# Values two to a step in odd pairs, a copied-out reciprocal, and the sums of a cross-attention folded on GpSimd

## The reference

```
x: (4, 256, 256)   context: (4, 4096, 256)   8 heads of 64
q  = ln(x) @ Wq1;  k, v = [ln(x) @ Wk1, context @ Wk2], [ln(x) @ Wv1, context @ Wv2]
attn = softmax(q k^T / 8 over 256 + 4096 keys);  out = (attn @ v) @ Wo + bo
```

## Time and profile before

| | |
|---|---|
| median of three runs | 1646.91 us (1642.55, 1646.91, 1647.23) |
| the profiled execution | 1643.33 us, its span 1641.8 us |
| mean granted TensorE clock | 0.962 of full speed |
| busy share of the span | TensorE 88%, VectorE 68%, GpSimd 64%, ScalarE 44% |
| units 1 to 14 of the cross-attention | from 131 to 1094 us of the span |
| the last unit | from 1094.4 to 1147.2 us |

### The profile page before, as it was taken

One profiled execution on the slowest core, in us unless ns is written; L12 is line 12 of the kernel. 1 busy time (PEld: TensorE's weight loads), 2 busy tenths in 40 slices (PEclk: granted clock), 3 DMA queues, 4 the chain that ended last, 5 costly groups with the idle time before them and its releaser, 6 DMA issues. The chain is left out here.

```text
span 1641.8 us, 27858 instructions
## 1 busy us (share of the span) xinstructions
PE 1449.9 (88%) x10964; PEld 1068.2 (65%) x10964; DVE 1124.3 (68%) x1299; ACT 728.3 (44%) x971; POOL 1049.4 (64%) x541
## 2 busy tenths in 40 slices
PE   4999999999999999999999999996597777827995
PEld 4767766776776776677677667664354444517995
DVE  2797578658658756855875785684776999644663
ACT  3454445534444544443554344342345333224773
POOL 3385469838547864754885665477134999443885
PEclk8999999999999999999999999998798999958998
DMA  5000021000003000001200000000304800092333
GB/s 176 14 11 11 1 87 49 1 14 21 2 27 88 24 2 14 21 1 39 88 11 14 10 11 1 1 2 1 85 19 190 214 0 1 1 368 62 63 60 59
DMA packets 62382, 76.39 MB, mean 47 GB/s; under 512 B 6384, under 2 KB 47984, under 8 KB 61856
## 3 DMA queue, kind: packets, MB, share of 16 engines
q1 hardware_dynamic: 57168, 68.51, 13.7%
q0 software_dynamic: 5088, 6.11, 2.5%
HBM read 58.39 MB, written 17.25 MB: 46 GB/s over the span
## 5 line engine op out<-in xcount | busy, mean ns | idle before, releaser
L393 POOL TENSOR_TENSOR xa_prob_sum<-xa_prob_sum,xa_probs 128x1024 f32<-128x1024 f32 x240 | 573.5, 2389 | 177.9 <-ACT xa_probs L481 158.7
L552 DVE TENSOR_REDUCE xa_maxes<-psum 128x2 f32<-128x1024 f32 (+1 forms) x288 | 334.2, 1162 | 240.1 <-PE psum L753 238.3
L481 ACT ACTIVATE xa_probs<-xa_probs 128x1024 f32<-128x1024 f32 x272 | 288.6, 1061 | 429.1 <-DVE xa_probs L574 428.8
L574 DVE TENSOR_TENSOR xa_probs<-psum,xa_max_rows 128x1024 f32<-128x1024 f32 x272 | 330.3, 1216 | 14.8 <-PE psum L784 8.5
L796 PE MATMUL psum<-xa_probs,xa_vals 128*64 128x256 f32 x2176 | 280.9, 389 | 4.0 <-ACT xa_probs L481 2.8
L796 PEld LDWEIGHTS psum<-xa_probs,xa_vals 128*64 128x64 f32 x2176 | 137.8, 136 | 106.4 <-issue 42.9
L780 PE MATMUL psum<-xa_q_hi,xa_k_hi 64*128 64x256 f32 x1088 | 158.8, 285 | 0.8 <-DVE xa_probs L574 0.8
L678 PE MATMUL psum<-xa_wv_hi,xa_ctx_hi 128*128 128x256 f32 x512 | 150.9, 295 | 7.8 <-DVE xa_maxes L552 7.8
L784 PE MATMUL psum<-xa_q_hi,xa_k_lo 64*128 64x256 f32 x1088 | 155.3, 279 | 0.0
L782 PE MATMUL psum<-xa_q_lo,xa_k_hi 64*128 64x256 f32 x1088 | 155.2, 279 | 0.0
L753 PE MATMUL psum<-xa_k_hi,xa_q_hi 64*128 64x512 f32 (+1 forms) x604 | 136.0, 452 | 21.4 <-DVE xa_maxes L552 9.3
(11 more groups left out here) (329 smaller groups left out, 2887.0 us busy)
## 6 DMA issues: line engine op xcount, KB each, us to landing
xa_ctx_in<-in_ctxT_dram SPq DMA_DIRECT2D x32, 512.0 KB, 4.6
ex_slots<-mx_blank_tile SPq DMA_DIRECT2D x2, 4372.5 KB, 38.4
xa_stage<-in_L_xattn_Wk_dram SPq DMA_DIRECT2D x32, 128.0 KB, 2.4
xa_stage<-in_L_xattn_Wv_dram SPq DMA_DIRECT2D x16, 256.0 KB, 3.0
ex_raw<-in_L_ffn_w_gate_dram SPq DMA_DIRECT2D x8, 512.0 KB
ex_raw<-in_L_ffn_w_up_dram SPq DMA_DIRECT2D x8, 512.0 KB
ex_raw<-in_L_ffn_w_down_dram SPq DMA_DIRECT2D x8, 512.0 KB
ex_xt<-ex_slots SPq DMA_DIRECT2D x15, 265.0 KB, 3.1
```

What stands on the lines that cost most here:

```text
L393: pool.tensor_tensor(prob_sum[:, :], prob_sum[:, :], probs[:, n % RING, :], ALU.add).then_inc(summed, 1)
L481: nc.scalar.activation(probs[:, n % RING, :], probs[:, n % RING, :], ACT.Exp, scale=HD ** -0.5).then_inc(exp_done, 1)
L552: dve.tensor_reduce(maxes[:, qt, :, g:g + 1], max_banks(v, g, qt)[:, :, 0:group_keys(g)[1]], AX_X, ALU.max).then_inc(max_reduced, 1)
L574: dve.tensor_tensor(probs[:, n % RING, :].rearrange("p (h t q) -> p h t q", h=2, t=2), S[:, 2 * (n % 2):2 * (n % 2) + 2, :].rearrange("p h ...
```

## The change

- `v_due`: an odd unit now makes 16 values in the steps 1 to 8, the even unit after it only the last one, in step 0.
- TensorE: in odd units `project_keys(v, d+1)` goes behind the values, to the end of the step, and both `weigh` stand ahead of the values. In step 8 the values stand ahead of `weigh(u, 16)`. In step 0 `sum_probs(u-1)` stands ahead of the value and of `project_keys(v, 1)`.
- VectorE: in odd units `split_keys(v, d)` stands behind the first `reduce_max` of the step, ahead of `shift(u, 2d)`. The reciprocal and `normalize` are taken in step 0 of even units, and in the steps 1 and 2 of odd ones. `split_q` stands ahead of `store_max`.
- The reciprocal comes from SBUF: ScalarE copies the bank O as a whole to `raw` (`store_outputs`, in step 0 between the two exponentials); `weigh(u, 0)` waits for this copy alone. `normalize` then has both its inputs in SBUF.
- GpSimd folds `prob_sum` in half once per unit (`fold_sums`, behind the last `add_probs`), so that `sum_probs` has two matmuls in place of four.
- In the last unit VectorE adds up every third tile (1, 4, 7, 10, 13, 16) by itself in `late_sum`; GpSimd adds the other eleven, unfolded, and `sum_probs` sums both.

```diff
+def late(j):
+    return j % 3 == 1
 def sums_done(n):
...
-    return n // HG * (HG - 1) + max(1, n % HG)
+    u, j = n // HG, n % HG
+    if u == U - 1:
+        return u * (HG - 1) + max(1, sum(not late(i) for i in range(j + 1)) - 1)
+    return u * (HG - 1) + max(1, j)
+def late_done(j):
+    return sum(late(i) for i in range(j + 1))
...
         prob_sum = sb("xa_prob_sum", [P, 2 * 2 * N1])
-        inv_sum = sb("xa_inv_sum", [P, N1])
+        raw = sb("xa_raw", [P, 2, N1])
         heads_T = sb("xa_heads_T", [P, IC, N1])
...
         bo_sb = heads_T[:, 0, :]
+        late_sum = xl_next[:, 0:4, :].rearrange("p t d -> p (t d)")
...
             if u % 2 == 1 and u + 1 < U:
-                return [((u + 1) // 2, j) for j in (2 * d - 4, 2 * d - 3) if 0 <= j]
+                return [((u + 1) // 2, j) for j in (2 * d - 2, 2 * d - 1) if 0 <= j]
             if u % 2 == 0 and u > 0:
-                return [(u // 2, j) for j in (2 * d + 14, 2 * d + 15) if j < HG]
+                return [(u // 2, HG - 1)] if d == 0 else []
             return []
...
+            def fold_sums(u):
+                both = prob_sum[:, :].rearrange("p (h t q) -> p h t q", h=2, t=2)
+                pool.wait_ge(summed, sums_done((u + 1) * HG - 1))
+                pool.tensor_tensor(both[:, :, 0, :], both[:, :, 0, :], both[:, :, 1, :], ALU.add).then_inc(folded, 1)
...
             for u, d in steps():
-                if d >= 1:
+                if d >= 1 and not (u == U - 1 and late(2 * d - 1)):
                     add_probs(u, 2 * d - 1)
...
                     split_weights(u + 2)
-                if d >= 1:
+                if d >= 1 and not (u == U - 1 and late(2 * d)):
                     add_probs(u, 2 * d)
+                if d == STEPS - 1 and u < U - 1:
+                    fold_sums(u)
                 if d == 3 and u % 2 == 0 and u + 2 < U:
...
                                      v_bank(c, j).rearrange("p (t e) -> p t e", t=2), ACT.Copy).then_inc(v_stored, 1)
+            def store_outputs(u):
+                act.wait_ge(sums_ready, u + 1)
+                act.wait_ge(pv_done, (u + 1) * HG)
+                if u > 0:
+                    act.wait_ge(o_normalized, u)
+                nc.scalar.activation(raw[:, :, :].rearrange("p a q -> p (a q)"), O, ACT.Copy).then_inc(o_stored, 1)
...
                 v = u + 1
-                if d == 0 and v < U:
-                    store_k_hi(v, 0)
-                    if own_due(u, d) is not None:
-                        store_own_hi(own_due(u, d))
+                following = v < U
+                chunk = chunk_due(u, d)
+                if d == 0:
+                    if following:
+                        store_k_hi(v, 0)
+                        if own_due(u, d) is not None:
+                            store_own_hi(own_due(u, d))
+                    exponentials(u, 0)
+                    if u > 0:
+                        store_outputs(u - 1)
+                    if chunk is not None:
+                        split_chunk(u // PAIRS + 1, chunk)
+                    exponentials(u, 1)
+                    for c, j in v_due(u, d):
+                        store_values(c, j)
+                    if following:
+                        store_k_hi(v, 1)
+                    continue
                 exponentials(u, 2 * d)
-                if d + 1 < NG and v < U:
-                    store_k_hi(v, d + 1)
-                if d < STEPS - 1:
+                if d == STEPS - 1:
+                    if u + 2 < U:
+                        store_q_hi(u + 2)
+                    for c, j in v_due(u, d):
+                        store_values(c, j)
+                    if chunk is not None:
+                        split_chunk(u // PAIRS + 1, chunk)
+                    if u + 2 < U:
+                        split_weights(u + 2)
+                    continue
+                if u % 2 == 0:
+                    if following:
+                        store_k_hi(v, d + 1)
                     exponentials(u, 2 * d + 1)
-                for c, j in v_due(u, d):
-                    store_values(c, j)
+                    if chunk is not None:
+                        split_chunk(u // PAIRS + 1, chunk)
+                else:
+                    if chunk is not None:
+                        split_chunk(u // PAIRS + 1, chunk)
+                    exponentials(u, 2 * d + 1)
+                    for c, j in v_due(u, d):
+                        store_values(c, j)
+                    if following:
+                        store_k_hi(v, d + 1)
                 if d == 3 and u % 2 == 0 and u + 2 < U:
                     split_values_weights(u // 2 + 1)
-                c = chunk_due(u, d)
-                if c is not None:
-                    split_chunk(u // PAIRS + 1, c)
                 if d == 6 and u + 2 < U:
                     split_query_weights(u + 2)
-                if d == STEPS - 1 and u + 2 < U:
-                    store_q_hi(u + 2)
-                    split_weights(u + 2)
...
                     dve.wait_ge(pv_done, n - RING + 1)
-                    dve.wait_ge(summed, sums_done(n - RING))
+                    if u == U - 1 and j >= RING and late(j - RING):
+                        dve.wait_ge(late_summed, late_done(j - RING))
+                    else:
+                        dve.wait_ge(summed, sums_done(n - RING))
                 dve.tensor_tensor(probs[:, n % RING, :].rearrange("p (h t q) -> p h t q", h=2, t=2),
...
             def invert_sums(u):
-                dve.wait_ge(sums_ready, u + 1)
-                dve.reciprocal(inv_sum[:, :], O[:, N1:2 * N1]).then_inc(sums_inverted, 1)
+                if u == U - 1:
+                    dve.wait_ge(sums_ready, u + 1)
+                    dve.reciprocal(raw[:, 1, :], O[:, N1:2 * N1]).then_inc(sums_inverted, 1)
+                else:
+                    dve.wait_ge(o_stored, u + 1)
+                    dve.reciprocal(raw[:, 1, :], raw[:, 1, :]).then_inc(sums_inverted, 1)
...
                     dve.wait_ge(out_projected, b)
-                dve.tensor_tensor(heads_T[:, p, :], O[:, 0:N1], inv_sum[:, :], ALU.mult).then_inc(o_normalized, 1)
+                dve.tensor_tensor(heads_T[:, p, :], O[:, 0:N1] if u == U - 1 else raw[:, 0, :], raw[:, 1, :],
+                                  ALU.mult).then_inc(o_normalized, 1)
+            def add_late(j):
+                n = (U - 1) * HG + j
+                dve.wait_ge(exp_done, n + 1)
+                if j == 1:
+                    dve.tensor_copy(late_sum, probs[:, n % RING, :]).then_inc(late_summed, 1)
+                else:
+                    dve.wait_ge(late_summed, late_done(j) - 1)
+                    dve.tensor_tensor(late_sum, late_sum, probs[:, n % RING, :], ALU.add).then_inc(late_summed, 1)
...
                 v = u + 1
+                following = v < U
                 if d == 0:
-                    if v < U:
+                    if following:
                         split_keys(v, 0)
...
                     shift(u, 0)
-                    if v < U:
+                    if following:
                         reduce_max(v, 0, 0)
                     shift(u, 1)
-                    if v < U:
-                        split_keys(v, 1)
+                    if u > 0 and u % 2 == 0:
+                        invert_sums(u - 1)
+                        normalize(u - 1)
                     continue
-                if v < U:
+                if following:
                     reduce_max(v, d - 1, 1)
-                if d == 1 and u > 0:
-                    invert_sums(u - 1)
-                    normalize(u - 1)
+                    if u % 2 == 1 or d == 1:
+                        split_keys(v, d)
                 shift(u, 2 * d)
-                if v < U:
+                if following:
                     reduce_max(v, d, 0)
...
                     shift(u, 2 * d + 1)
-                    if v < U:
+                    if u % 2 == 1 and d == 1:
+                        invert_sums(u - 1)
+                    if u % 2 == 1 and d == (2 if following else 1):
+                        normalize(u - 1)
+                    if following and u % 2 == 0:
                         split_keys(v, d + 1)
-                elif v < U:
+                elif following:
                     reduce_max(v, d, 1)
                     reduce_rows(v)
-                    store_max(v)
                     if u + 2 < U:
                         split_q(u + 2)
+                    store_max(v)
+                if not following:
+                    for j in (2 * d - 2, 2 * d - 1):
+                        if late(j):
+                            add_late(j)
+            add_late(HG - 1)
             invert_sums(U - 1)
...
                 if j == 0 and u > 0:
-                    pe.wait_ge(o_normalized, u)
+                    pe.wait_ge(o_stored, u)
                 for t in range(2):
...
             def sum_probs(u):
-                pe.wait_ge(summed, (u + 1) * (HG - 1))
```

(56 more changed lines are left out.)

## The result

The changed kernel takes **1634.77 us** (median of four runs, 1632.64 to 1636.36); the kernel before took 1646.97 beside it (four runs, 1642.55 to 1647.23). The ratio is 0.9931, 95% interval 0.9911 to 0.9952: faster by 0.7%, where 1651 was forecast. The profiled execution took 1636.36 us, its span 1634.6, against 1643.33 and 1641.8 before. That is 7.0 us less and not 12.2: the profiled execution of before was one of its fastest, that of the change the slowest of its four.

The account below looks back on a forecast made before the run. TensorE was taken to bound the kernel up to the last unit, GpSimd in it. Terms of +13.9 us up to the last unit and -8.5 in it gave +5.4; 1651 us was forecast, range 1638 to 1664.

Parts of the forecast that it names:

- the size of a step of an odd unit: TensorE, odd units: a step goes from 8.99 to 9.55 us, with values starting at 4.89 after a new wait.
- two signs of being wrong: The prediction would be wrong if odd steps are under 9.0 us, or the fold is ready when asked for.
- The waits of the values: Odd units: values wait for the second maximum, delayed by split_keys, 0.71 us in 42 steps; +30.0 and +4.5 us.
- The waits that go: TensorE's listed waits for maxima, stores, values and q before the last unit all vanish: -26.0 us.
- The fold: sum_probs at 14 unit turns: shorter ones save 6.2 us, but waiting for GpSimd's fold costs 16.2 us.
- The two SBUF inputs: normalize in step 0 of even units is locked out by a GpSimd addition: +5.7 us, bounds 0 and 10.
- Rival C: VectorE and GpSimd do not exclude each other: -5.7 us and the last unit at -11.5, giving 1642; chance 0.20.
- The last unit: Sharing additions between GpSimd and VectorE ends the last unit earlier: -8.5 us, bounds -5 and -12.
- The clock term: Last unit: the clock no longer falls while TensorE waits 6.4 us, which gives about 0.5 us more.
- B: Odd steps: the value does not wait for the second maximum; 1651 - 34 = 1617 us, chance 0.12.
- D: ScalarE's queue is held longer, half a microsecond more at 14 turns and an uncovered exponential: 1660 us, chance 0.13.
- E: Last unit gains nothing because VectorE's additions hold back its shifts: 1659 us, chance 0.05.

Follow-up runs that it names:

- e9: e7 with normalize(u-1) of even units moved from step 0 to behind the first shift of step 1: 1592.96 us, ratio 0.9686.
- e2: Kernel before with only the last unit's changes (late, add_late, two-part sum_probs): 1639.58 us, ratio 0.9955.
- e5: Changed kernel without VectorE's six additions on late_sum, so every third tile of the last unit is in no sum: 1633.12 us, ratio 0.992.
- e1: Changed kernel with split_keys(v, d) behind the second shift in steps 1 to 7 of odd units: 1610.31 us, ratio 0.9785.
- e10: e7 without fold_sums, so sum_probs has four matmuls and waits for the last addition: 1600.46 us, ratio 0.9732.
- e12: e9 with project_queries(u+2) ahead of the last score_for_max in step 8 of odd units, apart from the values: 1592.88 us, one run.
- e13: e9 without fold_sums, so sum_probs has four matmuls and waits for the last addition: 1593.97 us, ratio 0.9688.
- e6: Changed kernel with the first weigh ahead of maxA as its own block in steps 1 to 7 of even units: 1640.73 us, ratio 0.9965.
- e7: e1 with odd units' sum_probs(u-1) behind project_keys(v, 1), and ScalarE's store_outputs and chunk behind the second exponential and keys: 1602.73 us, ratio 0.9741.

## Why the prediction was wrong

**The step that failed** is the size of a step of an odd unit, "4.89 + 3.06 + 1.60 = 9.55", and with it "Without a wait that is 1.87 + 0.43 + 1.88 + 3.06 + 1.60 = 8.84". Its mechanism and its times up to 4.89 were right. Its last two terms were read off the order of before, in which the values were followed by `weigh` and the keys stood between maxA and `weigh`; in the new order values and keys are neighbours, and are 2.95 and 1.48. 0.23 us, in 49 steps, is 11.3 of the 14.7 us by which the units came out below the forecast, and enough to turn its +5.4 into a gain; of the rest 2.5 lie at the turns to even units and 0.8 in the odd ones. The prediction did count one block less to start, but took the price from `weigh` and kept the rows' others. Neither of its two signs of being wrong came (odd steps under 9.0 us, a fold that is ready): it failed by a size. In its sums two slips are small beside this: seven times 1.2 + 0.3 is 10.5 and not 10.3, and its own sum for the median is 1652.3, from which it went to 1651 without a reason.

**The waits of the values**: right in size too. The list has 30.9 in 49 steps (0.64 in most, 0.31 to 0.37 and 0.81 in step 1, where 0.4 and 1.0 were forecast), for 34.5. But the list counts from the modelled end of the last `weigh`, 4.25 into the step, and a block that follows without a wait starts about 0.07 ahead of that end, at 4.18 as the prediction had it. 49 times 0.07 is 3.4 of the 3.6.

**The waits that go**: all of them went, and the turns to even units were 2.5 us shorter than forecast. **The fold**: waits at all 14 turns, up to 1.7 us in the place named; 7.9 at the turns to odd units (8.5 forecast) and 5.3 at those to even ones. With the three waits of 0.44 of the value behind it, which the prediction had in this item, the even ones make 6.6 for 7.7. That is 1.1 of the turns' 2.5; where the other 1.4 lie was not separated. Its price was right, but not its worth: taking it away changed nothing.

**The two SBUF inputs**: right in sign, place and size. 5.7 was forecast for the even units, and e9 gives 6.0. The Trainium skill (SBUF — State Buffer, Who interferes with whom) says that such a pair locks each other out until the other is done; the trace agrees: `normalize` is 0.42 us alone and 1.97 beside a GpSimd addition, and that addition's like is 2.4 alone and 3.3 behind one of VectorE's. Rival C is refuted: of the rivals its 1642 lay nearest, but for a cause that the runs exclude.

**The last unit**: -8.5 forecast, of it 8.2 for the additions and about 0.5 for the clock; found -7.1, and -7.5 as a time (e2). The clock term was wrong: the output's four matmuls take 2.08 us before and 2.07 after, at a granted clock of 0.5 (1.2 GHz) in both. TensorE has waited 6.4 and 1.1 us for the sums and 2.3 for `normalize` ahead of them. In e5, where they start earlier, they run at full clock and take 1.13 us.

**The rivals**: B was near as a price (34 for removing the wait; e1 took 27.2 off the odd units and left 0.1 in each step) and wrong as a forecast of this kernel. D did not show: in the whole list TensorE waits for an exponential once, 1.2 us in the last unit. E is refuted by e2.

**Open.** Times differ by up to 6 us where nothing in the stretches does. From the last reciprocal of the cross-attention to the end, where all versions have the same instructions, the profiled executions take 494.5 to 500.5 us: 497.9 before, 497.4 in the change, about 495 in e9, e10, e12 and e13, and about 499.5 in e1, e5, e6 and e7. Step 1 of unit 0 starts 81.3 to 83.6 us into the span. No run here was made for it. Why a change of block costs 0.1 us, and whether other pairs are free, wasn't tried either; the evidence that queries and values are a cheap pair is a single run.

## What to carry to other kernels

Price a block by the pair it makes with its neighbour in the new order, and not by the interval it had in the old one: 0.1 us too much in two places of a step that runs 49 times turned the sign here. Before a block moves forward on one engine, write out when its input is ready in both orders. One 0.6 us instruction on VectorE ahead of the thing awaited cost 24.5 us here, over three times what the last unit gained. And judge the parts of a bundle alone: a last unit worth 7.5 us hid new waits of 49. Last, sum the parts in the trace before a difference of a few us in the time is given a cause: here such differences lay in part where no edit reached.

## What the hardware showed that was not expected

- Between matmul blocks that both use the full array (values to keys) no time is lost: 0.12 us from the last to the first, as within the block. With most other neighbours about 0.1 is lost on one side or on both, also from scores to a maximum, which have the same form.
- A 128x256 multiply on VectorE with both inputs in SBUF takes 0.42 us alone and 1.97 beside a GpSimd addition, though they touch different tiles.
- The loser can be GpSimd: its additions of 2.4 us take up to 3.34 when a VectorE addition comes first.
